# Summing the second block's outputs of a selective scan with accumulating DMAs, and giving GpSimd every third product of the first block

## The reference

```python
def scan_fn(carry, inp):
    h, v = carry
    dA_t, mi_t, C_t = inp
    v = BETA * v + mi_t            # momentum, BETA = 0.6
    h = dA_t * h + v               # one first-order recurrence per channel and state
    y_t = jnp.einsum('ben,bn->be', h, C_t)
    return ((h, v), y_t)
...
y = ys.transpose(1, 0, 2) + dp * xb
y = y * jax.nn.silu(z)
return jnp.einsum('ble,de->bld', y, ow)
```

## Time and profile before

| | |
|---|---|
| Time, median of 3 runs | 1186.22 us (1180.61 to 1186.47) |
| Profiled execution, span from the first to the last instruction | 1169.3 us |
| Its own device time | not recorded; 11.3 to 17.2 us beside the span, by the three times |
| First scan to end of the last scan, layer 0 | 510.3 to 698.9 us |
| First scan to end of the last scan, layer 1 | 775.0 to 964.6 us |
| PE / DVE / ACT / POOL busy over the span | 90% / 86% / 70% / 48% |

### The profile page before, as it was taken

One profiled execution on the slowest core, in us unless ns is written; L12 is line 12 of the kernel. 1 busy time (PEld: TensorE's weight loads), 2 busy tenths in 40 slices (PEclk: granted clock), 3 DMA queues, 4 the chain that ended last, 5 costly groups with the idle time before them and its releaser, 6 DMA issues. The chain is left out here.

```text
span 1169.3 us, 21209 instructions
## 1 busy us (share of the span) xinstructions
PE 1055.2 (90%) x7811; PEld 660.0 (56%) x7811; DVE 1000.8 (86%) x1335; ACT 815.2 (70%) x1621; POOL 563.6 (48%) x451
## 2 busy tenths in 40 slices
PE   6899999999999778989999998899999994799992
PEld 4222222222223233468888875468888883498992
DVE  5899999999994776979999995989999999767774
ACT  3279898999998545978887844988886851265561
POOL 5401440000001121049999992079998993265663
PEclk9779999999999897899999999899999997699997
DMA  5210101010000510102222210102222216311124
GB/s 158 65 43 15 29 16 29 15 29 16 15 2 2 140 42 3 57 19 91 91 94 88 91 55 3 57 19 91 92 90 80 101 56 241 48 38 42 42 49 119
DMA packets 45989, 69.30 MB, mean 59 GB/s; under 512 B 14030, under 2 KB 27342, under 8 KB 45888
## 3 DMA queue, kind: packets, MB, share of 16 engines
q1 hardware_dynamic: 40152, 60.62, 16.5%
q0 software_dynamic: 2496, 5.14, 1.7%
q10 hardware_dynamic: 3240, 2.20, 0.7%
HBM read 55.47 MB, written 9.13 MB: 55 GB/s over the span
## 5 line engine op out<-in xcount | busy, mean ns | idle before, releaser
L2168 PEld LDWEIGHTS m_pair<-filter_w,delta_x_t 128*128 128x128 f32 x2560 | 296.0, 192 | 36.4 <-issue 33.6
L2168 PE MATMUL m_pair<-filter_w,delta_x_t 128*128 128x112 f32 (+3 forms) x2560 | 299.6, 276 | 11.0 <-DVE m_pair L2178 5.0
L532 DVE TENSOR_REDUCE neg_max<-max_ps 128x1 f32<-128x1024 f32 x256 | 295.6, 1214 | 15.2 <-PE max_ps L521 14.9
L648 ACT ACTIVATE exp_scores<-score_k 128x512 f32<-128x512 f32 x512 | 270.8, 607 | 28.5 <-PE score_k L640 22.8
L2147 ACT ACTIVATE decay<-delta,a_log 128x1024 f32<-128x1024 f32 x128 | 145.8, 1142 | 75.1 <-DVE normed L2178 36.2
L521 PE MATMUL max_ps<-k_rows,q_rows 48*128 48x512 bf16 x512 | 163.0, 400 | 12.4 <-DVE neg_max L532 10.7
L2139 ACT ACTIVATE filter_w<-filter,b_t 128x112 f32<-128x112 f32 (+1 forms) x576 | 167.4, 374 | 0.0
L640 PE MATMUL score_k<-q_rows,k_rows 51*128 51x512 bf16 x512 | 163.0, 389 | 2.4 <-ACT exp_scores L648 0.6
L667 PE MATMUL av_ps<-exp_scores,v_cols 128*32 128x256 f32 x2048 | 158.2, 394 | 0.0
L2178 DVE TENSOR_TENSOR_SCAN m_pair<-decay,m_pair 128x1024 f32<-128x1024 f32 x64 | 145.8, 2279 | 1.6 <-PE m_pair L2168 1.2
L541 POOL CAST neg_max_parts<-neg_max 128x16 bf16<-128x16 f32 x16 | 3.1, 196 | 235.2 <-DVE neg_max L532 235.2
(11 more groups left out here) (317 smaller groups left out, 1531.3 us busy)
## 6 DMA issues: line engine op xcount, KB each, us to landing
c_row<-c_rows SPq DMA_DIRECT2D x64, 512.0 KB, 3.6
gate_up_all<-in_gate_up_w SPq DMA_DIRECT2D x8, 512.0 KB, 7.6
qk_parts<-part SPq DMA_DIRECT2D x12, 256.0 KB, 2.9
delta<-h_t SPq DMA_DIRECT2D x24, 128.0 KB, 2.3
q_rows<-qk_parts SPq DMA_DIRECT2D x91, 32.0 KB
down_all<-in_down_w SPq DMA_DIRECT2D x8, 256.0 KB, 7.7
moe_normed<-normed SPq DMA_DIRECT2D x4, 512.0 KB, 6.8
k_rows<-qk_parts SPq DMA_DIRECT2D x15, 96.0 KB
```

The costliest lines, as they stand in the source:

```text
L532: ve.tensor_reduce(nm[leg % 2][:, 4 * j + qt:4 * j + qt + 1], mps[:, bank:bank + 2, :].rearrange("p a q -> p (a q)"), AX_X, ALU.max, negat ...
L648: ac.activation(pt[a % 4][:, HEADS[r % 4], :], eps[:, bank, :], ACT.Exp, scale=SC).then_inc(*exped.up())
L2168: mm = pe.matmul(vps[blk][:, lo:hi], self.duT[b][:, c, blk * P:(blk + 1) * P], wf[g % 3][:, lo:hi], start=True, stop=True)
```

## The change

1. **Second block's sum.** GpSimd still forms the product (L2205), now into two tiles `yq` in turn. The add on GpSimd (L2207) goes; in its place GpSimd issues a DMA that adds the 512 KB product onto `yacc[b]` in SBUF. Before it issues one, it waits until the previous state's accumulating DMA has landed, since both read and write the same sum (in the first state of a sequence it waits for the skip term instead).
2. **First block's product in states of k = 2.** DVE scans into the SBUF tile `h0s` instead of the PSUM tile, and GpSimd, not DVE, multiplies it by the C row. The other two of three stay on DVE.
3. **Order on GpSimd in a state of k = 2**: product of block 0, pair sum, product of block 1, wait, DMA. In other states: product of block 1, wait, DMA.
4. **Waits that follow.** The last gates and `ve_last` wait for a DMA's landing where they waited for GpSimd's add. C rows wait for the product of either engine.
5. **Rooms and semaphores.** `yq[1]` is made by widening `bc_rows` from 32 to 128 partitions; `h0s` lies in a spent modulation row. Four `couple_start` and four `rms_square` semaphores become one each, with counts, which frees semaphores for the DMAs.

```diff
+        self.yp, self.yq = places[:3], [normed[:, S:], self.bc_room[:]]
+        self.h0s = self.mrow[0][:].rearrange("p b i d -> p (b i d)")[:, 0:S]
...
         def ve_scan(b, n, blk):
...
-            wait_from(ve, (ys, yg)[blk].sem, g - blk)
-            ve.tensor_tensor_scan((hps[:], hh[g % 2])[blk], da[u % 4], vps[blk][:], 0.0, ALU.mult, ALU.add).then_inc(*hs.up())
+            on_po = kind(b, n) == 2
+            if blk:
+                wait_from(ve, yg.sem, g - 1)
+            elif on_po in h0_read:
+                ve.wait_ge(*h0_read[on_po])
+            ve.tensor_tensor_scan((h0s if on_po else hps[:], hh[g % 2])[blk], da[u % 4], vps[blk][:], 0.0, ALU.mult, ALU.add).then_inc(*hs.up())
...
-        def ve_output(b, n):
+        def first_output(b, n):
 
             g, k = state(b, n), kind(b, n)
+            engine, h, step = (po, h0s, yg0) if k == 2 else (ve, hps[:], ys)
...
+            engine.tensor_tensor(yp[k], h, csb[g % 3][:], ALU.mult).then_inc(*step.up())
+            first_y[g] = h0_read[k == 2] = step.at()
+
+        def po_output(b, n):
+
+            g = state(b, n)
+            to = added[g % 2]
+            po.wait_ge(c_in[g % 3].sem, 16 * (g // 3 + 1))
+            po.wait_ge(hs.sem, NBLK * g + 2)
+            if g - 2 in yacc_at:
+                po.wait_ge(*yacc_at[g - 2])
+            po.tensor_tensor(yq[g % 2], hh[g % 2], csb[g % 3][:], ALU.mult).then_inc(*yg.up())
+            po.wait_ge(yg.sem, g + 1)
+            if n:
+                po.wait_ge(*yacc_at[g - 1])
+            else:
+                po.wait_ge(*skip_at[b])
+            po.dma_start(yacc[b], yq[g % 2], accum_op=ALU.add).then_inc(*to.up(16))
+            yacc_at[g] = to.at()
...
-            po.tensor_tensor(yp_last, hh[g % 2], csb[g % 3][:], ALU.mult).then_inc(*yg.up())
-            po.wait_ge(yg.sem, g + 1)
-            po.tensor_tensor(yacc[b], yacc[b], yp_last, ALU.add).then_inc(*added.up())
...
-            for m in ((c_in[g % 3].sem, 16 * (g // 3 + 1)), (hs.sem, NBLK * g + 2), added.at()):
+            for m in ((c_in[g % 3].sem, 16 * (g // 3 + 1)), (hs.sem, NBLK * g + 2), yacc_at[g - 1]):
...
-            ended = self.s_last.at() if (l, b) == (NL - 1, NB - 1) else (added.sem, state(b, DS - 1) + 1)
+            ended = self.s_last.at() if (l, b) == (NL - 1, NB - 1) else yacc_at[state(b, DS - 1)]
```

More of the change, by code:

```diff
@@ L992, in coupling @@
         beta_step, couple_step = self.sig("beta_step"), self.sig("couple_step")
-        started = [self.sig(f"couple_start{c}") for c in range(NC)]
+        start_step, started = self.sig("couple_start"), {}
         swapped = [self.sig(f"swapped{c}") for c in range(NC)]
@@ L1103, in ve_start @@
             ve.scalar_tensor_tensor(out=chunk(c), in0=V[c], scalar=beta[:, c // 2:c // 2 + 1], in1=chunk(c),
-                                    op0=ALU.mult, op1=ALU.add).then_inc(*started[c].up())
+                                    op0=ALU.mult, op1=ALU.add).then_inc(*start_step.up())
+            started[c] = start_step.at()
         def ve_couple(c):
@@ L1340, in mamba_memory @@
         self.dr = sb("delta_low", [3 * R2 + DTR + 1, S])
-        self.bcr = sb("bc_rows", [R2, S])
+        self.bc_room = sb("bc_rows", [P, S])
+        self.bcr = self.bc_room[0:R2, :]
         self.ddiag = sb("d_diag", [P, P])
@@ L1351, in mamba_memory @@
         normed = self.N[:].rearrange("p a d -> p (a d)")
-        self.yp, self.yp_last = places[:3], normed[:, S:]
+        self.yp, self.yq = places[:3], [normed[:, S:], self.bc_room[:]]
+        self.h0s = self.mrow[0][:].rearrange("p b i d -> p (b i d)")[:, 0:S]
         self.hh = [normed[:, 0:S], self.HT[:, 0:S]]
         self.yacc = [self.HT[:, S:2 * S], places[3]]
-        self.rms_square, self.rms_sum = [self.sig(f"rms_square{c}") for c in range(NC)], self.sig("rms_sum")
+        self.rms_square, self.rms_sum, self.squared = self.sig("rms_square"), self.sig("rms_sum"), {}
         self.tap_step, self.rate_step, self.pad_step = self.sig("tap_step"), self.sig("rate_step"), self.sig("pad_step")
@@ L1367, in mamba_memory @@
         self.s_ys, self.s_ysum, self.s_gated = (self.sig(n) for n in ("y_mul", "y_sum", "y_gated"))
-        self.s_yg, self.s_yacc, self.s_skip, self.s_pair, self.s_last = (
-            self.sig(n) for n in ("y_mul_g", "y_add_g", "skip_g", "y_pair", "y_last"))
+        self.s_yg, self.s_yg0, self.s_skip, self.s_last = (
+            self.sig(n) for n in ("y_mul_g", "y_mul_g0", "skip_g", "y_last"))
+        self.s_yacc = [self.sig(f"y_add_dma{k}") for k in range(2)]
+        self.s_pair = self.sig("y_pair")
         self.c_in = [self.sig(f"c_in{k}") for k in range(3)]
@@ L2111, in mamba_scan @@
         wset, vmm, decay, hs = self.s_w, self.s_v, self.s_decay, self.s_hs
-        ys, yg, added, skip = self.s_ys, self.s_yg, self.s_yacc, self.s_skip
+        ys, yg, yg0, added, skip = self.s_ys, self.s_yg, self.s_yg0, self.s_yacc, self.s_skip
         ysum, gated, c_in = self.s_ysum, self.s_gated, self.c_in
@@ L2115, in mamba_scan @@
         csb, da, hh, yacc, yp, wf, tri = self.csb, self.da, self.hh, self.yacc, self.yp, self.wf, self.tri
-        yp_last, pair = self.yp_last, self.s_pair
-        yp_read = {}
+        yq, h0s, pair = self.yq, self.h0s, self.s_pair
+        yp_read, first_y, h0_read, yacc_at = {}, {}, {}, {}
         G0 = l * NB * DS
@@ L2127, in sp_c_row @@
             g = state(b, n)
-            wait_from(sp, ys.sem, g - 2)
+            if g - G0 >= 3:
+                sp.wait_ge(*first_y[g - 3])
             wait_from(sp, yg.sem, g - 2)
@@ L2180, in kind @@
         def kind(b, n):
             return (b * DS + n) % 3
-        def ve_output(b, n):
+        def first_output(b, n):
             g, k = state(b, n), kind(b, n)
-            ve.wait_ge(c_in[g % 3].sem, 16 * (g // 3 + 1))
-            ve.wait_ge(hs.sem, NBLK * g + 1)
+            engine, h, step = (po, h0s, yg0) if k == 2 else (ve, hps[:], ys)
+            engine.wait_ge(c_in[g % 3].sem, 16 * (g // 3 + 1))
+            engine.wait_ge(hs.sem, NBLK * g + 1)
             if k in yp_read:
-                ve.wait_ge(*yp_read[k])
-            ve.tensor_tensor(yp[k], hps[:], csb[g % 3][:], ALU.mult).then_inc(*ys.up())
+                engine.wait_ge(*yp_read[k])
+            engine.tensor_tensor(yp[k], h, csb[g % 3][:], ALU.mult).then_inc(*step.up())
+            first_y[g] = h0_read[k == 2] = step.at()
@@ L2193, in po_pair @@
         def po_pair(b, n):
-            po.wait_ge(ys.sem, state(b, n) + 1)
+            po.wait_ge(*first_y[state(b, n) - 1])
+            po.wait_ge(*first_y[state(b, n)])
             po.tensor_tensor(yp[1], yp[1], yp[2], ALU.add).then_inc(*pair.up())
             yp_read[2] = pair.at()
[L2199 to L2204, removed]
-            po.tensor_tensor(yp_last, hh[g % 2], csb[g % 3][:], ALU.mult).then_inc(*yg.up())
-            po.wait_ge(yg.sem, g + 1)
-            po.tensor_tensor(yacc[b], yacc[b], yp_last, ALU.add).then_inc(*added.up())
@@ L2226, in pe_sums @@
             if k == 1:
-                pe_sum(0, (ys.sem, state(b, n)), b > 0 and n == 0)
+                pe_sum(0, first_y[state(b, n) - 1], b > 0 and n == 0)
             if (b, n) == states[-1]:
-                pe_sum(k, (ys.sem, state(b, n) + 1), True)
+                pe_sum(k, first_y[state(b, n)], True)
         def ve_last(b, n):
```

16 lines of the change are left out of this document (9 added, 7 removed).

## The result

The changed kernel takes 1244.22 us (median of 5 runs, 1240.07 to 1252.03); the kernel before, now over 5 runs, 1180.61 us (1175.61 to 1186.47). The ratio is 1.0549, 95% interval 1.0506 to 1.0592: 5.5% slower, about 64 us. The forecast was 38 us slower. Runs that record both show that the device time lies only a little above the span, 1.3 us in the changed kernel (1252.03 beside 1250.7) and about 1.7 us in the kernel before (1171.34 beside 1169.7). So the profiled execution of before took about 1171 us, faster than all five above, and the profiled one of after is the slowest of its five. The spans are therefore not compared whole, but stage by stage.

The account below looks back on a forecast made before the run. PE was taken to set the pace, at a floor of 17.21 us per three states. Late landings cost 17.1 and 21.3 us in the two layers, together 38.4, swallowing DVE's 4.3 us gain: 1224.6 us, range 1182 to 1262.

Parts of the forecast that it names:

- The bound now: Scan stages: PE sets the pace, its floor 17.21 us per three states against 17.30 measured, DVE within 0.1 us.
- The gain on DVE: Scans: one product in three leaves DVE, gaining 1.8 us over about 20 turns of three states and 2.5 in state 17.
- The wait for the last landing: GpSimd in the scans: each accumulating DMA waits for the previous landing, GpSimd idle meanwhile; hidden only for flights up to 4.3 us.
- k = 2 step: GpSimd, from DMA to DMA into a k = 2 state: issue plus three instructions and gaps, 8.45 us, covering the flight.
- The size of a waiting step: GpSimd, from DMA to DMA into the other two states: flight plus 0.1 us, 5.6 us each.
- L: Time from issue to landing of a 512 KB accumulating DMA: bounded between 4.3 and 7.4 us, taken as 5.5.
- Which wait it turns into: Scans: DVE's second-block scans would wait for GpSimd's product, DVE's busy share falling under 0.85.
- Costs at the ends: Layer ends: last gates wait for a landing, layer 0 ending 17.1 us late and layer 1 21.3, all exposed.
- hidden, PE sets the pace: Rival for the scans: flights at most 4.4 us stay hidden, 1180 to 1188 us; chance 0.30.
- the break-even of the prediction: Scans: the flight time up to which 8.65 us plus two flights stays hidden below 17.2 us: 4.3 us.
- DVE set the pace after all: Rival for the scans: each turn of three states shrinks by up to 1.14 us, 25 us in all, 1161 us; chance 0.04.

Follow-up runs that it names:

- e6: The kernel before, with DVE's first-block product left out in states of k = 2: 1173.98 against 1174.03 us, ratio 1.0014.
- e7: The changed kernel with four product tiles and two sums, each DMA waiting for the landing two before, DVE adding the sums: 1187.24 us, ratio 1.0130 to the kernel before.
- e3: The changed kernel with plain copies in place of the accumulating DMAs: ratio 0.9985 to the kernel before.
- e4: The changed kernel with C rows loaded only for the first three states of each layer: ratio 1.0188 to the kernel before.
- e5: The changed kernel with each accumulating DMA taking only half of the columns: ratio 1.0096 to the kernel before.
- e1: The changed kernel with all of the first block's products kept on DVE, accumulating DMAs staying: 1192.38 us, ratio 1.0154 to the kernel before.

## Why the prediction came out as it did

**The bound now: right, and shown.** PE's 4.85 us through momentum, scan, momentum is the floor (e6).

**The gain on DVE: 4.3 us predicted, none found.** Both terms were too kind. In the steady turn the 0.09 us between the floor of 17.21 and 17.30 don't belong to the product. In state 17 the product's 1.23 us were taken off the turn as if DVE alone decided it. e6 shows the turn unchanged, since the gate ends 1.1 us after GpSimd's pair sum with or without the product.

**The wait for the last landing: right.** e7 loosens it, and the turn is 17.3 again. The k = 2 step was put at 8.45 us and is 8.4.

**The size of a waiting step: mis-sized.** The prediction put it at L + 0.1, 5.6 us. The 20 such steps of layer 0 average 6.08 us (half at about 7.0, half at 5.0) and the 19 of layer 1 6.40 (some of the short ones are 5.7 to 6.9 there). At 0.5 to 0.8 us more for each of 39 steps this is 25 us: the difference between the 38.4 predicted and the 63.2 found. By the flights of the same 39 DMAs, 5.5 us on average in layer 0 and 5.8 in layer 1, some 18 of the 25 us are the hand-over, which was put at 0.1 and measures 0.5 to 0.6, and only 7 are L.

**L itself: right by luck.** Its 5.5 was added up from a copy of 4.3, 0.8 for half of a second read, and 0.4 for a quarter of a C row. The runs show 2.9 for a quiet copy (e3), 1.6 more for adding, and 2.0 in every second such flight for C rows (e4), 1.0 on average: 5.5. An error of -1.4 hid two of +0.8 and +0.6.

**Which wait it turns into: partly wrong.** The prediction had DVE's second block scans waiting for GpSimd's product. The lateness goes another way, through the pair sum to PE and from there to DVE's products and scans.

**Costs at the ends: right in layer 1, not in layer 0.** `ve_last` waits 4.0 us for a landing, and the second gate of state 17 in layer 1 waits 1.6. The last gate of layer 0 waits for none: its DMA, issued at 738.90, landed after 4.5 us, at 743.4, and the gate starts at 744.32, 7.34 us behind the first gate (736.98) just as in the kernel before (699.76 and 707.10). The first gate had waited for PE's last sum, so the lateness of 27.2 us, where 17.1 were predicted, reached this end through the pair sums and PE.

**The rival "hidden, PE sets the pace"** is what happens in e3 (ratio 0.9985), where flights of 5.5 and 2.9 us alternate and all of them average 4.3, the break-even of the prediction. With the steps as measured that break-even is 3.9 (8.4 + 2 x 0.5 + 2L under 17.2), so e3 lies slightly above it, e5 (4.4), e4 (4.7) and the change (5.7) further. The rival "DVE set the pace after all" is excluded by e6.

The forecast of 1224.6 us came from a median of before of 1186.22; over five runs it was 1180.61.

Open: the part behind the last gate, 1 to 9 us longer on the changed kernel. The scans of the two layers took 20.2 us longer in e1 and 10.3 in e7, beside 18.4 and 13.2 between the medians, so a few us of e7 are not placed. Where the gate's 5.7 us (e1) go, beyond that GpSimd's two instructions cover them, was not separated. Splitting the C row's issue from the product's end was not tried.

## What to carry to other kernels

An accumulating DMA takes an add off an engine, but a sum built by such DMAs is a chain of landings: price it as flights in series, each with the cost of adding, with a hand-over from landing to next issue (0.5 us here), and with whatever else the same event releases. Before moving work off an engine that looks full, leave the work out and time that: here it showed in one run that the engine had nothing to give. And when a chain has lag, time removed elsewhere is not won; it only lets the chain show.

## What the runs showed of the hardware

- A 512 KB accumulating DMA from GpSimd within SBUF: issue 0.89 us, landing 4.5 us after the start of the issue when no C row was issued with it, 6.5 us when two 512 KB loads fell into its flight. The next issue that waited for it began 0.5 us after the landing. A plain copy: issue 0.59, landing 2.9. Half a tile: 3.3.
- An accumulating DMA of 512 KB took 2.7 us of all 16 DMA engines, a plain copy 1.3, a C row 1.6.
- A DVE instruction with two SBUF inputs (1.22 us alone) took 5.70 us beside two GpSimd instructions that ran back to back, which took 2.67 and 2.64. In the kernel before, the two shared the loss, 1.79 to 2.44 on DVE and 3.33 to 3.35 instead of 2.36 on GpSimd. The Trainium skill (SBUF — State Buffer, "Who interferes with whom") states the contention, and that the order of issue decides who stands still. e1's gate, which began 0.35 us after GpSimd's instruction and stood still, agrees.
- After 4.96 us of idleness PE's granted clock was 0.50 (1.2 GHz) and its next 20 passes took 4.58 us instead of 2.3: the 4.5 us that the gate lost on DVE cost PE another 2.3.
